# GpSimd makes the product of gate and up, and the product with the block scales, in the feed-forward pass of an adaLN block

## The chip, the cores and the metric

One core of one Trainium2 chip. The metric is the device time of one execution in microseconds, the median of the runs; lower is better. The engines are TensorE (PE), VectorE (DVE), ScalarE (ACT), GpSimd (POOL) and SyncE (SP), which issues all DMAs here. Everything is float32.

## What is computed

`x` is 16 sequences (batches) of 512 tokens with 128 features. A modulation vector per batch scales and shifts two normalised inputs: one of an attention block (chunked ridge attention with a rank-8 subspace), one of a feed-forward block with blockwise FP4 quantisation. The change touches the feed-forward block:

```
def fp4_quant_dequant(x):            # blocks of 16 along the last dim
    scale = max(max|xb| / 6, 1e-12)
    q = GRID[searchsorted(MID, |xb / scale|)] * sign * scale

gate = fp4_linear(h, w_gate)         # 128 -> 352
y    = fp4_linear(h, w_up)           # 128 -> 352
out  = fp4_linear(silu(gate) * y, w_down)   # quantised again, 352 -> 128
x    = x + gb * out
```

with `h = layernorm(x) * (1 + cb) + sb`.

## The kernel before

The kernel runs three passes one after the other. `front_pass` makes the modulation and the normalised inputs of attention; `attention_pass` makes the attention block and, towards its end, the quantised feed-forward inputs of the first 12 batches; `ffn_pass` makes the feed-forward inputs of the last 4 batches (its "hidden" group, `HiddenInput`) and then the feed-forward block of all 16.

In `ffn_pass` one batch is a tile of 128 partitions x 4 token groups (NC), each with 352 hidden features (FI) in 22 blocks of 16. A batch goes through these steps:

- `gate_up(b)`: TensorE transposes the input (L648), ScalarE copies it out of PSUM (L601), TensorE multiplies with gate and up weights, token group by token group (L654, L655), in two PSUM banks each. ScalarE empties each with Silu into `sg` (L606) and with Copy into `up` (L607), which increments `up_ok`. TensorE may fill a bank again when ScalarE has emptied it.
- `combine(b)` on VectorE: waits for four `up_ok` of batch b, makes `hh = sg * up` (L697, 128x1408), then quantises `hh` in place in two halves of 704 elements with `fp4_blocks`: the largest magnitude of each block (L459), scale (L460), reciprocal (L461), product with it (L462), the rounding step from the exponent bits (L463, L464), add and subtract it (L465, L466), product with the scale (L469), which increments `hhq_ok`, once for each half.
- `down(b)`: TensorE waits for both halves (`hhq_ok`), transposes `hh` in three chunks (L663), ScalarE copies each out (L612, in `turned`), TensorE multiplies with the down weights (L670) into `p_y`.
- `finish(b)` on VectorE: waits for `p_y`, multiplies with `gb` (L692) and adds `x` (L693). SyncE stores the result (L566) and then loads the batch three ahead (L560 to L562).

Every engine works through its own instructions in the order in which they are written; semaphores join them. TensorE's and ScalarE's order is gate_up(0), gate_up(1), and then for each b: down(b) (ScalarE: turned(b)), gate_up(b+2). VectorE's order is the hidden group, and then for each b: combine(b), finish(b-1). GpSimd has only the identity, a constant and the reciprocal square root of the hidden group (`hidden.pool`, L118 and L120); after that it has nothing to do in this pass. In the attention pass it makes two elementwise operations of 128x512 for each batch (L1432, L1434).

`sg`, `up`, `hh`, `hht` and `ys` have two buffers, taken in turn by batch; the inputs `x`, `gb` and `h` have four. The scales and the other quantisation buffers have one each, cut in two halves.

Of the kernel before, what the change touches and what calls it, by code (L numbers as in the profile page):

```python
# [29 lines left out]
ALU = mybir.AluOpType  # L30
# [3 lines left out]
P = 128  # L34
B = 16
NC = 4
# [11 lines left out]
FI = 352  # L48
QB = 16
NBF = D // QB  # L50
NBI = FI // QB
# [38 lines left out]
def make_identity(nc, pool, ident, sem, count, value=1.0):  # L90

    nc.gpsimd.memset(ident, 0.0).then_inc(sem, 1)
    pool.wait_ge(sem, count + 1)
    nc.gpsimd.affine_select(out=ident, in_=ident, compare_op=ALU.not_equal, fill=value, base=0,
                            pattern=[[-1, ident.shape[1]]], channel_multiplier=1).then_inc(sem, 1)


def bcast(ap, dim, n):

    a = ap.unsqueeze(dim)  # L100
    shape = list(a.shape)
    shape[dim] = n
    return a.to_broadcast(shape)
# [79 lines left out]
def front_pass(nc, x, ln_g, ln_b, c, wmod, s_mod, s_c, s_xnt, s_base):  # L183

    with ExitStack() as ctx:
# [31 lines left out]
        STORES = 16 * 3  # L217
        LOOPS = (B - 1 - 2) // S

        def batches(eng, step_):  # L220

            step_(0, 0)
            with eng.Fori(0, LOOPS) as k:
                for i in range(S):
                    step_(k * S + (i + 1), (i + 1) % S)
            for b in range(1 + LOOPS * S, B):
                step_(b, b % S)
# [5 lines left out]
        with nc.Block() as block:  # L233
# [133 lines left out]
            def _(dve):  # L367
# [35 lines left out]
                def step_(b, s):  # L403
                    if exists(b, 2):
                        stats(b + 2, (s + 2) % S, 0)
                    if exists(b, 1):
                        make_h(b + 1, (s + 1) % S)
                        stats(b + 1, (s + 1) % S, 1)
                    product = make_base(b, s)
                    if exists(b, 2):  # L410
                        neg_mean(b + 2, (s + 2) % S, 0)
                    make_xn(b, s, product)
                    if exists(b, 1):
                        neg_mean(b + 1, (s + 1) % S, 1)
# [17 lines left out]
                first = ch.n  # L432
                with dve.Fori(0, LOOPS) as k:
                    ch.base, ch.n = k * (S * STEP_LINKS), first
                    for i in range(S):
                        step_(k * S + (i + 1), (i + 1) % S)
                    assert ch.n - first == S * STEP_LINKS, ch.n - first
                ch.base, ch.n = LOOPS * (S * STEP_LINKS), first
                for b in range(1 + LOOPS * S, B):
                    step_(b, b % S)  # L440

def fp4_blocks(nc, ch, jobs):

    last = {}  # L450

    def each(instruction, first=False):
        for k, job in enumerate(jobs):
            if not first:
                ch.wait(last[k])
            last[k] = ch.inc(instruction(*job[:5]))

    V = nc.vector
    each(lambda v, amax, scale, inv, step: V.tensor_reduce(amax, v, op=ALU.max, axis=AX_X, apply_absolute_value=True), first=True)  # L459
    each(lambda v, amax, scale, inv, step: V.tensor_scalar(scale, amax, 1.0 / 6.0, 1e-12, ALU.mult, ALU.max))  # L460
    each(lambda v, amax, scale, inv, step: V.reciprocal(inv, scale))  # L461
    each(lambda v, amax, scale, inv, step: V.tensor_tensor(v, v, bcast(inv, 2, QB), ALU.mult))  # L462
    each(lambda v, amax, scale, inv, step: V.tensor_scalar(step.bitcast(I32), v.bitcast(I32), 0x7F800000, None, ALU.bitwise_and))  # L463
    each(lambda v, amax, scale, inv, step: V.tensor_scalar(step, step, 1.0, 1.5 * 2.0 ** 22, ALU.max, ALU.mult))  # L464
    each(lambda v, amax, scale, inv, step: V.tensor_tensor(v, v, step, ALU.add))  # L465
    each(lambda v, amax, scale, inv, step: V.tensor_tensor(v, v, step, ALU.subtract))  # L466
    for k, (v, amax, scale, inv, step, done) in enumerate(jobs):
        ch.wait(last[k])
        V.tensor_tensor(v, v, bcast(scale, 2, QB), ALU.mult).then_inc(done, 1)  # L469


def fp4_weights(nc, ch, v, rows, nb, tmp):
# [25 lines left out]
def ffn_pass(nc, s_wgu, s_wdn, s_mod, s_x1, s_h, out):  # L498


    with ExitStack() as ctx:
        sb = lambda name, shape, dt=F32: ctx.enter_context(nc.sbuf_tensor("m_" + name, shape, dt))
        ps = lambda name, shape: ctx.enter_context(nc.psum_tensor("m_" + name, shape, F32))
        sem = lambda name: ctx.enter_context(nc.semaphore("m_" + name))
# [7 lines left out]
        S = 4  # L512
# [4 lines left out]
        sg = [sb(f"sg{s}", [P, NC, FI]) for s in range(2)]  # L517
        up = [sb(f"up{s}", [P, NC, FI]) for s in range(2)]
        hh = [sb(f"hh{s}", [P, NC, FI]) for s in range(2)]
        hht = [sb(f"hht{s}", [P, NW, NC, P]) for s in range(2)]  # L520
        ys = [sb(f"y{s}", [P, NC, D]) for s in range(2)]
        q_hh = [sb(n, [P, NC * NBI]) for n in ("amax", "scale", "inv")] + [sb("step", [P, NC * FI])]
        late_x, late_md = sb("late_x", [P, GB_N, NC, D]), sb("late_md", [P, GB_N, 2, D])
        late_step, late_small = sb("late_step", [P, GB_N * NC * D]), sb("late_small", [P, 2 * BANK])
        hidden = HiddenInput(nc, sem, [late_x[:]], [late_md[:]], late_step[:], lambda at, n: late_small[:, at:at + n], nhalf[:])
# [7 lines left out]
        x_in = [sem(f"x_in{s}") for s in range(S)]  # L533
        saved = [sem(f"saved{s}") for s in range(2)]
        nhalf_ok, dve_chain, passed = (sem(n) for n in ("nhalf_ok", "dve_chain", "passed"))
        ht_mm, ht_ok, gate_mm, up_ok, hh_ok, hhq_ok, hht_mm, hht_ok, y_mm, y_ok = (
            sem(n) for n in ("ht_mm", "ht_ok", "gate_mm", "up_ok", "hh_ok", "hhq_ok", "hht_mm", "hht_ok", "y_mm", "y_ok"))

        AHEAD = 3
        LOOPS = (B - 1 - AHEAD) // S  # L540

        def batches(eng, step_):

            step_(0, 0)
            with eng.Fori(0, LOOPS) as k:
                for i in range(S):
                    step_(k * S + (i + 1), (i + 1) % S)
            for b in range(1 + LOOPS * S, B):
                step_(b, b % S)

        def exists(b, ahead):

            return not isinstance(b, int) or b + ahead < B

        with nc.Block() as block:
# [34 lines left out]
            @block.gpsimd  # L590
            def _(pool):
                make_identity(nc, pool, ident[:], ident_ok, 0)
                nc.gpsimd.memset(nhalf[:], -0.5).then_inc(nhalf_ok, 1)
                pool.wait_ge(nhalf_ok, 1)
                hidden.pool(pool, 0)

            @block.scalar
            def _(act):
# [84 lines left out]
            @block.vector  # L683
            def _(dve):
                ch = Chain(dve, dve_chain)
                for s in range(2):
                    dve.sem_inc(saved[s], 16)

                def finish(b, s):
                    dve.wait_ge(y_mm, b + 1)  # L690
                    dve.wait_ge(saved[s % 2], (b - s % 2) * 8 + 16)
                    ch.link(nc.vector.tensor_tensor(ys[s % 2][:], p_y[:], gb[s][:].to_broadcast([P, NC, D]), ALU.mult))  # L692
                    nc.vector.tensor_tensor(ys[s % 2][:], ys[s % 2][:], xs[s][:], ALU.add).then_inc(y_ok, 1)  # L693

                def combine(b, s):
                    dve.wait_ge(up_ok, b * NC + NC)
                    nc.vector.tensor_tensor(hh[s % 2][:], sg[s % 2][:], up[s % 2][:], ALU.mult).then_inc(hh_ok, 1)  # L697
                    dve.wait_ge(hh_ok, b + 1)
                    jobs = []
                    for half in range(2):  # L700
                        nb = NC * NBI // 2
                        amax, scale, inv = (x[:, half * nb:(half + 1) * nb] for x in q_hh[:3])
                        v = hh[s % 2][:, half * NC // 2:(half + 1) * NC // 2].rearrange("p t (b k) -> p (t b) k", k=QB)
                        step = q_hh[3][:, half * nb * QB:(half + 1) * nb * QB].rearrange("p (b k) -> p b k", k=QB)
                        jobs.append((v, amax, scale, inv, step, hhq_ok))
                    fp4_blocks(nc, ch, jobs)


                STEP_LINKS = 2 * 8 + 1

                def step_(b, s):
                    combine(b, s)
                    if not isinstance(b, int) or b >= 1:
                        finish(b - 1, (s - 1) % S)

                hidden.vector(dve, ch, 0, 0, passed)
                step_(0, 0)
                first = ch.n
                with dve.Fori(0, LOOPS) as k:
                    ch.base, ch.n = k * (S * STEP_LINKS), first  # L720
                    for i in range(S):
                        step_(k * S + (i + 1), (i + 1) % S)
                    assert ch.n - first == S * STEP_LINKS, ch.n - first
                ch.base, ch.n = LOOPS * (S * STEP_LINKS), first
                for b in range(1 + LOOPS * S, B):
                    step_(b, b % S)
                finish(B - 1, (B - 1) % S)
# [898 lines left out]
```

## Time and profile before

| what | us |
|---|---|
| median of 3 runs | 1955.35 |
| lowest and highest | 1954.31, 1958.24 |
| span of the profiled execution | 1955.5 |
| VectorE busy | 1637.0 (84%) |
| TensorE busy | 1111.4 (57%) |
| ScalarE busy | 796.1 (41%) |
| GpSimd busy | 120.1 (6%) |
| mean granted TensorE clock | 0.767 |
| first instruction of the down product's pass on batch 0 (L663) | at 1736.91 |

The span is the time from the first to the last instruction of one profiled execution, and the busy shares are of that span. The timeline lists instructions in order of time, with their start and duration in us; like instructions are merged, with their count behind x. What stands in brackets is the idle time of the engine before them and what ended it. In the answers on windows, each stretch has its length, the busy time of PE, PEld (TensorE's weight loads), DVE, ACT and POOL with their instruction counts, the granted TensorE clock (1.00 is 2.4 GHz, 0.50 is 1.2 GHz), the DMA share and GB/s.

### The profile page before, as it was taken

The page shows a single profiled execution, that of the slowest core. Times are in us where ns is not written, and L with a number is a line of the kernel's source. Part 1 is how long each engine was busy: PE and PEld are TensorE (multiplying, and loading weights), DVE is VectorE, ACT ScalarE, POOL GpSimd, SP SyncE. Part 2 cuts the span into 40 slices and gives each one's busy share as a digit, 9 for nine tenths or more (in the row PEclk, how much of TensorE's full clock was granted, in tenths as well). Part 3 has the DMA queues.
Part 4 walks back from the last instruction along what each step waited for, and adds up shares of the span by engine and source line. Part 5 has one row for each costly group of instructions (what it writes and reads, how often), then busy time and mean ns, then how long its engine had stood idle before and what let it go on. Part 6 is the DMA issues. An engine that isn't in the chain of part 4 may idle for free. (4 is left out here: it accounts for less than half of the span.)

```text
span 1955.5 us, 54893 instructions
## 1 busy us (share of the span) xinstructions
PE 1111.4 (57%) x21470; PEld 912.4 (47%) x21470; DVE 1637.0 (84%) x5229; ACT 796.1 (41%) x1499; POOL 120.1 (6%) x119
## 2 busy tenths in 40 slices
PE   2438201891662876776486867377407717347876
PEld 1325101851552863575485456277306616235554
DVE  6865799699999489999939999976998970399997
ACT  3645100652541553673354465255406404124342
POOL 3530000000000002000001100000201000200000
PEclk6659655695895688898669889758758959579998
DMA  2551000000000002100000200000121110411220
GB/s 91 173 182 57 27 0 0 15 29 12 3 3 1 4 3 81 35 4 3 2 4 24 81 2 4 2 3 4 61 78 43 39 39 2 132 51 57 66 64 28
DMA packets 58236, 73.85 MB, mean 38 GB/s; under 512 B 4512, under 2 KB 32880, under 8 KB 57984
## 3 DMA queue, kind: packets, MB, share of 16 engines
q1 hardware_dynamic: 57984, 70.38, 11.4%
q8 instruction: 172, 2.82, 0.6%
q14 instruction: 80, 0.66, 0.1%
HBM read 44.61 MB, written 25.76 MB: 36 GB/s over the span
## 5 line engine op out<-in xcount | busy, mean ns | idle before, releaser
L1500 DVE TENSOR_TENSOR a_blocks<-a_blocks,a_outer 128x384 f32<-128x384 f32 (+3 forms) x1024 | 455.3, 487 | 0.0
L1494 DVE TENSOR_TENSOR a_outer<-a_blocks,a_scaled 128x128 f32<-128x128 f32 (+3 forms) x1024 | 440.7, 492 | 2.0 <-DVE a_blocks L1528 1.3
L1150 ACT ACTIVATE a_pair<-a_bank 32x512 f32<-32x512 f32 (+1 forms) x352 | 207.2, 592 | 205.6 <-PE a_bank L932 126.5
L932 PE MATMUL a_bank<-a_ident,a_blocks 128*128 128x128 f32 x256 | 46.8, 367 | 366.7 <-DVE a_blocks L1510 366.7
L1150 ACT ACTIVATE a_work<-a_bank 32x512 f32<-32x512 f32 (+1 forms) x224 | 130.7, 589 | 294.5 <-PE a_bank L932 222.9
L932 PEld LDWEIGHTS a_bank<-a_ident,a_blocks 128*128 128x128 f32 x256 | 45.3, 214 | 368.3 <-DVE a_blocks L1510 197.8
L883 PE MATMUL a_bank<-a_wk,a_cg 128*128 128x512 f32 x256 | 123.6, 630 | 11.5 <-issue 11.5
L951 PE MATMUL a_bank<-a_work,a_gram 64*32 64x32 f32 (+1 forms) x4096 | 105.8, 220 | 17.9 <-issue 14.7
L951 PEld LDWEIGHTS a_bank<-a_work,a_gram 64*32 64x32 f32 (+1 forms) x4096 | 98.6, 135 | 23.4 <-issue 21.4
L1150 ACT ACTIVATE a_xb<-a_bank 128x512 f32<-128x512 f32 x112 | 63.4, 596 | 112.4 <-PE a_bank L1056 63.8
L1432 POOL TENSOR_TENSOR a_xc<-a_xc,a_ga 128x512 f32<-128x512 f32 x16 | 23.2, 1453 | 1358.2 <-ACTq L1155 1311.6
L1150 ACT ACTIVATE a_xa<-a_bank 128x512 f32<-128x512 f32 x112 | 62.3, 604 | 65.2 <-PE a_bank L1056 43.7
L1563 DVE TENSOR_TENSOR a_basis<-a_basis,a_dinv 128x512 f32<-128x512 f32 x8 | 5.2, 688 | 91.4 <-PEq L1099 91.4
L883 PEld LDWEIGHTS a_bank<-a_wk,a_cg 128*128 128x128 f32 x256 | 48.8, 200 | 68.0 <-issue 61.8
L1056 PE MATMUL a_bank<-a_pair,a_ya 64*8 64x64 f32 x4096 | 51.9, 227 | 45.8 <-issue 35.0
L895 PEld LDWEIGHTS a_bank<-a_pair,a_wk 128*64 128x64 f32 x1024 | 55.5, 137 | 38.1 <-ACT a_pair L1150 38.1
L109 DVE BATCH_NORM_STATS2 m_late_small<-m_late_x 128x6 f32<-128x128 f32 x16 | 3.4, 274 | 83.2 <-DMA m_late_md<-s_mod 83.2
L895 PE MATMUL a_bank<-a_pair,a_wk 128*64 128x128 f32 x1024 | 62.1, 275 | 16.0 <-ACT a_pair L1150 16.0
L951 PE MATMUL a_bank<-a_pair,a_work 64*32 64x64 f32 x2048 | 68.0, 224 | 5.1 <-issue 4.1
L951 PEld LDWEIGHTS a_bank<-a_pair,a_work 64*32 64x32 f32 x2048 | 62.8, 111 | 7.5 <-issue 5.9
L1056 PEld LDWEIGHTS a_bank<-a_pair,a_ya 64*8 64x8 f32 x4096 | 42.1, 86 | 48.5 <-issue 48.1
L351 PE MATMUL f_pt<-f_ident,f_xn 128*128 128x128 f32 x64 | 17.4, 425 | 79.9 <-DVE f_xn L398 77.7
(212 smaller groups left out, 2625.5 us busy)
## 6 DMA issues: line engine op xcount, KB each, us to landing
f_x<-in_L_attn_x SPq DMA_DIRECT2D x16, 256.0 KB, 3.2
s_xnt<-f_xt SPq DMA_DIRECT2D x16, 256.0 KB, 2.1
s_c<-f_cm SPq DMA_DIRECT2D x16, 256.0 KB, 2.3
s_base<-f_base SPq DMA_DIRECT2D x16, 256.0 KB, 2.8
a_cg<-s_c SPq DMA_DIRECT2D x16, 256.0 KB, 2.7
a_cc<-s_c SPq DMA_DIRECT2D x16, 256.0 KB, 3.6
a_xnt<-s_xnt SPq DMA_DIRECT2D x16, 256.0 KB, 3.7
a_base_in<-s_base SPq DMA_DIRECT2D x16, 256.0 KB, 2.7
```

What stands on the lines that cost most here:

```text
L109: ch.inc(nc.vector.bn_stats(raw[:, t], x[:, t]))
L351: last = nc.tensor.transpose(p_t[s % 2][:, t], ns[s][:, t], ident[:])
L883: last = nc.tensor.matmul(bank[:], cg[bb % 2][:, 2 * (tp % 2) + i], wk[:, 8 * half:8 * half + 8, :].rearrange("p h d -> p (h d)"), start=T ...
L895: last = nc.tensor.matmul(bank[rows(s, None), i * P:(i + 1) * P].rearrange("p (t c) -> p t c", t=2), wk[:, h, :], ck[tp % 2][:, :, h * DH: ...
L932: last = nc.tensor.transpose(bank[:, i * P:(i + 1) * P], rows_[:, :, 4 * jb + i], ident[:])
L951: last = nc.tensor.matmul(two[s][at(s), i * w:(i + 1) * w], stationary, moving, start=True, stop=True)
L1056: last = nc.tensor.matmul(two[s][32 * c:32 * c + R, i * DH:(i + 1) * DH], src[rows(s, None), q, :], pair[rows(s, None), q, :], start=True, ...
L1150: nc.scalar.activation(out, view, ACT.Copy, scale=scale).then_inc(emptied, 1)
L1432: nc.gpsimd.tensor_tensor(y, y, ga[:].to_broadcast([P, NC, D]), ALU.mult).then_inc(pool_chain, 1)
L1494: made[a] = ch.inc(V.tensor_tensor(outer[a // KEPT], bcast(factor, 3, HB - a), bcast(scaled[:, :, a:HB], 2, KEPT), ALU.mult))
L1500: differences = ch.inc(V.tensor_tensor(strip, strip, outer[a // KEPT], ALU.subtract))
L1563: last = V.tensor_tensor(basis[:, :, s], basis[:, :, s], bcast(dinv[:, s], 2, DH), ALU.mult)
```

## The change

The product of gate and up moves from VectorE to GpSimd, and so does the last step of the quantisation, the product with the scales. VectorE's `combine` becomes `quantise`, which waits for GpSimd's product (`hh_ok`), rounds both halves, and increments `rounded` once for each half. GpSimd's step b makes the product of batch b+1 and then, for each half of batch b, waits for `rounded` and multiplies with the scale; product 0 comes before the first step. The scales get two buffers, taken in turn by batch. All other engines keep their order.

```
--- before.py
+++ after.py
@@ -441,7 +441,7 @@
 
 
 
-def fp4_blocks(nc, ch, jobs):
+def fp4_blocks(nc, ch, jobs, rounded=None):
 
 
 
@@ -466,7 +466,10 @@
     each(lambda v, amax, scale, inv, step: V.tensor_tensor(v, v, step, ALU.subtract))
     for k, (v, amax, scale, inv, step, done) in enumerate(jobs):
         ch.wait(last[k])
-        V.tensor_tensor(v, v, bcast(scale, 2, QB), ALU.mult).then_inc(done, 1)
+        if rounded is None:
+            V.tensor_tensor(v, v, bcast(scale, 2, QB), ALU.mult).then_inc(done, 1)
+        else:
+            ch.eng.sem_inc(rounded, 1)
 
 
 def fp4_weights(nc, ch, v, rows, nb, tmp):
@@ -519,7 +522,8 @@
         hh = [sb(f"hh{s}", [P, NC, FI]) for s in range(2)]
         hht = [sb(f"hht{s}", [P, NW, NC, P]) for s in range(2)]
         ys = [sb(f"y{s}", [P, NC, D]) for s in range(2)]
-        q_hh = [sb(n, [P, NC * NBI]) for n in ("amax", "scale", "inv")] + [sb("step", [P, NC * FI])]
+        q_amax, q_inv, q_step = sb("amax", [P, NC * NBI]), sb("inv", [P, NC * NBI]), sb("step", [P, NC * FI])
+        q_scale = [sb(f"scale{s}", [P, NC * NBI]) for s in range(2)]
         late_x, late_md = sb("late_x", [P, GB_N, NC, D]), sb("late_md", [P, GB_N, 2, D])
         late_step, late_small = sb("late_step", [P, GB_N * NC * D]), sb("late_small", [P, 2 * BANK])
         hidden = HiddenInput(nc, sem, [late_x[:]], [late_md[:]], late_step[:], lambda at, n: late_small[:, at:at + n], nhalf[:])
@@ -533,11 +537,18 @@
         x_in = [sem(f"x_in{s}") for s in range(S)]
         saved = [sem(f"saved{s}") for s in range(2)]
         nhalf_ok, dve_chain, passed = (sem(n) for n in ("nhalf_ok", "dve_chain", "passed"))
+        rounded = sem("rounded")
         ht_mm, ht_ok, gate_mm, up_ok, hh_ok, hhq_ok, hht_mm, hht_ok, y_mm, y_ok = (
             sem(n) for n in ("ht_mm", "ht_ok", "gate_mm", "up_ok", "hh_ok", "hhq_ok", "hht_mm", "hht_ok", "y_mm", "y_ok"))
 
         AHEAD = 3
         LOOPS = (B - 1 - AHEAD) // S
+
+        def half_of(s, half):
+
+            nb = NC * NBI // 2
+            v = hh[s % 2][:, half * NC // 2:(half + 1) * NC // 2].rearrange("p t (b k) -> p (t b) k", k=QB)
+            return v, q_scale[s % 2][:, half * nb:(half + 1) * nb]
 
         def batches(eng, step_):
 
@@ -593,6 +604,24 @@
                 nc.gpsimd.memset(nhalf[:], -0.5).then_inc(nhalf_ok, 1)
                 pool.wait_ge(nhalf_ok, 1)
                 hidden.pool(pool, 0)
+
+                def product(b, s):
+                    pool.wait_ge(up_ok, b * NC + NC)
+                    nc.gpsimd.tensor_tensor(hh[s % 2][:], sg[s % 2][:], up[s % 2][:], ALU.mult).then_inc(hh_ok, 1)
+
+                def rescale(b, s):
+                    for half in range(2):
+                        pool.wait_ge(rounded, b * 2 + (half + 1))
+                        v, scale = half_of(s, half)
+                        nc.gpsimd.tensor_tensor(v, v, bcast(scale, 2, QB), ALU.mult).then_inc(hhq_ok, 1)
+
+                def step_(b, s):
+                    if exists(b, 1):
+                        product(b + 1, (s + 1) % S)
+                    rescale(b, s)
+
+                product(0, 0)
+                batches(pool, step_)
 
             @block.scalar
             def _(act):
@@ -692,24 +721,22 @@
                     ch.link(nc.vector.tensor_tensor(ys[s % 2][:], p_y[:], gb[s][:].to_broadcast([P, NC, D]), ALU.mult))
                     nc.vector.tensor_tensor(ys[s % 2][:], ys[s % 2][:], xs[s][:], ALU.add).then_inc(y_ok, 1)
 
-                def combine(b, s):
-                    dve.wait_ge(up_ok, b * NC + NC)
-                    nc.vector.tensor_tensor(hh[s % 2][:], sg[s % 2][:], up[s % 2][:], ALU.mult).then_inc(hh_ok, 1)
+                def quantise(b, s):
                     dve.wait_ge(hh_ok, b + 1)
                     jobs = []
                     for half in range(2):
                         nb = NC * NBI // 2
-                        amax, scale, inv = (x[:, half * nb:(half + 1) * nb] for x in q_hh[:3])
-                        v = hh[s % 2][:, half * NC // 2:(half + 1) * NC // 2].rearrange("p t (b k) -> p (t b) k", k=QB)
-                        step = q_hh[3][:, half * nb * QB:(half + 1) * nb * QB].rearrange("p (b k) -> p b k", k=QB)
-                        jobs.append((v, amax, scale, inv, step, hhq_ok))
-                    fp4_blocks(nc, ch, jobs)
+                        amax, inv = (x[:, half * nb:(half + 1) * nb] for x in (q_amax, q_inv))
+                        v, scale = half_of(s, half)
+                        step = q_step[:, half * nb * QB:(half + 1) * nb * QB].rearrange("p (b k) -> p b k", k=QB)
+                        jobs.append((v, amax, scale, inv, step, None))
+                    fp4_blocks(nc, ch, jobs, rounded)
 
 
                 STEP_LINKS = 2 * 8 + 1
 
                 def step_(b, s):
-                    combine(b, s)
+                    quantise(b, s)
                     if not isinstance(b, int) or b >= 1:
                         finish(b - 1, (s - 1) % S)
 
```

## Rows read from the trace of the kernel before

**Rows 1.** The page: the span, and each engine's busy time.
```profile
span 1955.5 us, 54893 instructions
...
PE 1111.4 (57%) x21470; PEld 912.4 (47%) x21470; DVE 1637.0 (84%) x5229; ACT 796.1 (41%) x1499; POOL 120.1 (6%) x119
```

**Rows 2.** The chain of waits in the last pass: start us, us, what.
```profile
1753.02 1.64 DVE m_hh L697
...
1764.42 0.88 DVE m_hh L469
...
1930.54 1.55 DVE m_hh L697
```

**Rows 3.** The timeline of VectorE over one batch.
```profile
1766.54 1.62 DVE L697 TENSOR_TENSOR m_hh<-m_sg,m_up 128x1408 f32<-128x1408 f32 x1
...
1768.20 1.68 DVE L459 TENSOR_REDUCE m_amax<-m_hh 128x44 f32<-128x704 f32 x2
...
1777.13 1.69 DVE L469 TENSOR_TENSOR m_hh<-m_hh,m_scale 128x704 f32<-128x704 f32 x2
...
1778.73 0.68 DVE L692 TENSOR_TENSOR m_y<-m_py,m_gb 128x512 f32<-128x512 f32 x1
...
1780.06 1.62 DVE L697 TENSOR_TENSOR m_hh<-m_sg,m_up 128x1408 f32<-128x1408 f32 x1
```

**Rows 4.** The same timeline: the down product and the last evacuation of gate and up.
```profile
1768.10 2.94 PE L670 MATMUL m_py<-m_w_dn,m_hht 128*128 128x128 f32 x24 [0.68 <-ACT m_hht L612]
...
1777.64 0.46 ACT L607 ACTIVATE m_up<-m_pu 128x352 f32<-128x352 f32 x1
```

**Rows 5.** The timeline of GpSimd in the attention pass, its last group.
```profile
1660.37 1.26 POOL L1432 TENSOR_TENSOR a_xc<-a_xc,a_ga 128x512 f32<-128x512 f32 x1 [112.33 <-ACTq L1155]
1661.71 1.26 POOL L1434 TENSOR_TENSOR a_xc<-a_xc,a_base_in 128x512 f32<-128x512 f32 x1
```

**Rows 6.** The timeline of VectorE and GpSimd, attention pass: a meeting, and the same alone.
```profile
743.70 2.76 DVE L1494 TENSOR_TENSOR a_outer<-a_blocks,a_scaled 128x384 f32<-128x384 f32 x4
744.26 1.46 POOL L1432 TENSOR_TENSOR a_xc<-a_xc,a_ga 128x512 f32<-128x512 f32 x1 [600.56 <-ACTq L1155]
...
755.74 1.70 DVE L1494 TENSOR_TENSOR a_outer<-a_blocks,a_scaled 128x384 f32<-128x384 f32 x4
```

**Rows 7.** Windows and the timeline of TensorE at the last batch.
```profile
1934.90:1942.70 7.80, 0.00 (x0) 0.00 (x0) 7.80 (x13) 0.00 (x0) 0.00 (x0) 0.63 0.00 0
1942.70:1949.00 6.30, 5.54 (x24) 4.86 (x25) 1.31 (x3) 1.79 (x3) 0.00 (x0) 0.50 0.14 42
...
1942.78 2.89 PE L663 MATMUL m_phht<-m_ident,m_hh 128*128 128x128 f32 x12 [7.89 <-DVE m_hh L469]
...
1946.35 4.95 PE L670 MATMUL m_py<-m_w_dn,m_hht 128*128 128x128 f32 x24 [0.68 <-ACT m_hht L612]
```

**Rows 8.** The timeline of the first batch after the hidden group.
```profile
1735.16 1.69 DVE L469 TENSOR_TENSOR m_hh<-m_hh,m_scale 128x704 f32<-128x704 f32 x2
...
1736.91 2.89 PE L663 MATMUL m_phht<-m_ident,m_hh 128*128 128x128 f32 x12 [22.80 <-DVE m_hh L469]
...
1740.48 5.47 PE L670 MATMUL m_py<-m_w_dn,m_hht 128*128 128x128 f32 x24 [0.68 <-ACT m_hht L612]
...
1747.77 0.76 PE L655 MATMUL m_pu<-m_w_gu,m_ht 128*128 128x352 f32 x2
...
1752.53 0.46 ACT L607 ACTIVATE m_up<-m_pu 128x352 f32<-128x352 f32 x1
```

**Rows 9.** The timeline of gate and up of batches 0 and 1.
```profile
1703.17 1.38 PE L654 MATMUL m_pg<-m_w_gu,m_ht 128*128 128x352 f32 x2
...
1706.37 0.76 PE L654 MATMUL m_pg<-m_w_gu,m_ht 128*128 128x352 f32 x2
...
1708.11 0.46 ACT L607 ACTIVATE m_up<-m_pu 128x352 f32<-128x352 f32 x1
...
1714.51 0.46 ACT L607 ACTIVATE m_up<-m_pu 128x352 f32<-128x352 f32 x1
```

## The prediction

> **What bounds the kernel now.** The page comes first: VectorE is busy 84% of a span of 1955.5 us, TensorE 57%, GpSimd 6% [rows 1]. These are averages over three passes, and the change touches only the last one, so the chain of waits of that pass is read next. It shows what the engines hand each other batch by batch: the chain comes back to the product of gate and up (L697) at 1753.02 for batch 2 and at 1930.54 for batch 15 [rows 2]. These thirteen steps take 177.5 us, 13.65 each; an ordinary one is 13.52.
>
> The timeline of VectorE in one batch shows why [rows 3]. It has no gap: 1.66 us from the product to the first reduction, 8.93 from there to the first product with the scales (L469), 1.60 for the two of those, 1.33 for the finish of the batch before. Sum 13.52. So VectorE sets the period in the middle of the pass.
>
> How much room do the others have? The same batch on TensorE and ScalarE [rows 4]: after the quantised product is complete (L469 ends at 1765.30 [rows 2]), TensorE transposes it, multiplies (L670), and goes on to gate and up of the batch two ahead; ScalarE empties the last bank of that at 1778.10. That is 12.80 us, against a period of 13.52. The reader is to see that this leg, from the end of batch b's rescaling to the end of batch b+2's gate and up, is nearly as long as the period. It is hidden only because it runs beside VectorE's work on batch b+1.
>
> **The change, part by part.**
>
> *VectorE is relieved* of 1.66 + 1.60 = 3.26 us a batch; for the new completion wait and two semaphore increments I give back 0.1. It would need 10.36 us a batch.
>
> *GpSimd's prices.* The trace has no GpSimd product of 1408 or 704 elements. The nearest are the 128x512 products of the attention pass, 1.26 us undisturbed, the one that follows through a semaphore 0.08 after the end of the first [rows 5]. When such an operation meets VectorE, four VectorE products that take 1.70 alone take 2.76 [rows 6]: 1.06 us is shut-out, which I take as the part that grows with the size, and 0.20 as fixed. Then 1408 elements cost 2.75 x 1.06 + 0.20 = 3.12 us, 704 elements 1.375 x 1.06 + 0.20 = 1.66. With everything growing in proportion they would be 3.47 and 1.73; with the fixed part only they could not be less than 3.12 and 1.66. I take the low ones. L1432 has an operand repeated over whole rows of 128, L1434 none, both 1.26; repetition inside blocks of 16 is in no row, and at worst I let it double the rescale.
>
> *The order on GpSimd* is the step that decides. Its step b first waits for all of gate and up of batch b+1 and makes product b+1, and only then rescales batch b. GpSimd takes its work in order, so the rescale of b, however early VectorE has rounded it, stands behind that wait. And gate and up of b+1 is issued on TensorE behind down(b-1), which waits for the rescale of b-1. That closes a loop with one batch per turn: rescale b-1 done, down(b-1), gate and up of b+1, product b+1, rescale b. In the kernel before, TensorE's leg lay beside VectorE's work on the batch in between; now nothing on GpSimd lies beside it. VectorE's quantising of b is no part of the loop: it starts when product b is there, some 3.5 us ahead of the loop's start, and ends long before product b+1. Who waits: TensorE for the rescale, VectorE for product b+1, SyncE's stores and ScalarE behind TensorE.
>
> GpSimd's share of a turn: 0.08 + 3.12 + 0.08 + 1.66 + 0.08 + 1.66 = 6.68 us. With the leg at 12.80 the turn would be 19.48.
>
> *The clock of that leg.* In every turn TensorE would idle during GpSimd's share and ScalarE's last two evacuations (0.46 each, L607 in rows 4), about 7.6 us. The trace has one idle time of that length behind busy work: 7.89 us before the last batch. The granted clock averages 0.63 in it and is 0.50 when the work resumes; the 24 products of L670 take 4.95 us [rows 7] where they take 2.94 at full clock [rows 4]. The first batch, too, begins at half clock, after 22.80 us of idleness: L469 ends at 1736.85, L670 takes 5.47, and then gate and up runs at full clock to 1752.99 [rows 8]. That leg is 16.14 us, 3.34 more, and it is the pattern I expect in each turn: down at 1.2 GHz, gate and up at 2.4. The turn is 16.14 + 6.68 = 22.82 us.
>
> *Contention.* At product b+1 VectorE has nothing to do, and the rescale of b meets the two reductions of b+1 and then its first two-input product. I cost this at nothing inside the loop; if the two took turns for VectorE's products, it would add 0.8 us a turn.
>
> The Trainium skill (SBUF — State Buffer, Who interferes with whom) says that a VectorE instruction with two SBUF inputs and a GpSimd instruction that reads SBUF shut each other out for a whole instruction, and that reductions don't. The trace agrees for the first half, 2.76 against 1.70 us. By that rule alone the change would give the third rival below; by the order on GpSimd it gives 22.82 a turn, and the shut-outs fall where VectorE idles.
>
> **The sum**, on the profiled execution. Batches 0 and 1 have gate and up ready at 1708.57 and 1714.97 [rows 9], while VectorE still prepares the last group. The two early products shut VectorE out there by 0 to 2 x 2.92; I take 3.7, since part falls on a reduction. VectorE's first product (1.65) goes. Rounding of batch 0 ends at 1735.16 - 1.65 + 3.7 = 1737.2, and the rescale (0.08 + 1.66 + 0.08 + 1.66 = 3.48) ends at 1740.7; before, that was 1736.85. Fourteen turns, for b = 1 to 14: + 319.5, 2060.2. Batch 15 has no product behind it: its quantising starts 3.48 before that, takes 8.93 and one shut-out of 1.46, and its rescale 3.48: + 10.4, 2070.6. After so short a gap I take full clock for its down: 5.74 (1765.30 to 1771.04 in rows 2 and 4), then 4.2 as before from the end of L670 at 1951.30 to the end [rows 7]. Total 2080.5, say 2081, 125 us over the span. The profiled span stands 0.15 us from the median of the runs, so nothing is corrected.
>
> **The rivals.**
>
> *The loop with TensorE at full clock.* If idle times of 7.6 us don't lower the clock, the turn is 19.48 and the end 2034. Against it: the fall inside 7.89 us.
>
> *The loop with gate and up at half clock too.* A pair of L654 takes 1.38 us before the clock rises and 0.76 after [rows 9]; eight pairs of L654 and L655 add 5.0, the turn is 27.8, the end 2151. Against it: the clock had risen when gate and up ran, 11 us after the work's resumption: a pair of L655 takes 0.76 there [rows 8].
>
> *Contention decides, not order.* If gate and up of b+1 came early enough, VectorE's 10.36 plus at most 2.92 + 2 x 1.46 of shut-outs would be 16.2 us a batch, 2.7 more than now, and 15 batches end at 1996. For it speaks the 1.06 us per operation; against it the order.
>
> *Faster.* If the rescale never stood behind a wait, VectorE at 10.36 would cease to bind and TensorE's leg of 12.80 would: 0.7 less in fourteen batches, 1945. It takes gate and up of b+1 to be there before VectorE has rounded b. That is so for batches 0 and 1 only; from b = 2 the leg is 12.8 behind the rescale of b-1 and rounding b is done about 7 behind it.
>
> *GpSimd dearer in blocks of 16.* Doubled rescales add 3.3 a turn: 2130.
>
> **How the numbers follow.** Forecast 0.66, full clock 0.10, half clock throughout 0.07, contention 0.04, faster 0.03, dearer rescale 0.10. The forecast's own range is 2055 to 2105: 0.3 a turn less for an earlier rise of the clock, the start without shut-outs; 0.5 more for products in proportion and 0.8 for turns with VectorE. The range 2030 to 2135 takes in full clock and the dearer rescale and leaves out 0.14. The measurement tells 0.2%, about 4 us. Faster 0.03, same 0.01, slower 0.96.
>
> **What would show it.** GpSimd's timeline: product, rescale, rescale back to back, then idle for some 16 us on ScalarE's L607, with periods near 22.8; products near 3.1 us, rescales near 1.7. L663 waits for GpSimd, L459 too, VectorE idle nearly half of each period. L670 near 5.4 us and L654 pairs near 0.76. Wrong would be: rescales that start right when VectorE has rounded; periods below 17 us; L670 at 2.9; GpSimd operations stretched beyond 4 us beside busy VectorE.

## The result, and the profile after

The changed kernel takes 2049.47 us (median of 4 runs, 2046.22 to 2050.12) against 1956.0 for the kernel before (median of 4; the table of the time before has three of them): a ratio of 1.0483, 95% interval 1.0465 to 1.0501. It is slower by 4.8%, some 94 us. The forecast was 2081 with a range of 2030 to 2135. The span of the profiled execution is 2047.9 us.

First the page of the changed kernel, span and busy time, against [rows 1]:

```profile
span 2047.9 us, 54959 instructions
...
PE 1117.3 (55%) x21470; PEld 917.8 (45%) x21470; DVE 1605.9 (78%) x5181; ACT 797.5 (39%) x1499; POOL 215.4 (11%) x167
```

VectorE is busy for 31 us less (time in which one of its instructions is held up by GpSimd counts as busy), GpSimd for 95 us more, and the span is 92 us longer. The work that was moved is off the engine that bound the pass; what grew is waiting. The waits of the last pass say which engine waits for which (each line names the engine and line that waited, then the engine and line waited for, then us in total, times, longest):

```profile
POOL m_hh L610 <- ACT m_up L636: 207.2, 14, 16.1
DVE m_amax L459 <- POOL m_hh L610: 118.7, 14, 8.9
...
PE m_phht L692 <- POOL m_hh L616: 100.2, 15, 6.9
```

In the changed kernel L610 is GpSimd's product, L616 its rescale, L692 the transposes (L663 before), L699 the down product (L670), L636 the last evacuation (L607). GpSimd waits 14 times for ScalarE, 207.2 us in all; meanwhile VectorE waits 118.7 us for GpSimd's product and TensorE 100.2 for its rescale. The timeline of GpSimd gives the order of events:

```profile
1816.26 3.15 POOL L610 TENSOR_TENSOR m_hh<-m_sg,m_up 128x1408 f32<-128x1408 f32 x1 [15.48 <-ACT m_up L636]
1819.37 2.73 POOL L616 TENSOR_TENSOR m_hh<-m_hh,m_scale 128x704 f32<-128x704 f32 x2
1835.87 3.15 POOL L610 TENSOR_TENSOR m_hh<-m_sg,m_up 128x1408 f32<-128x1408 f32 x1 [13.77 <-ACT m_up L636]
1838.97 2.73 POOL L616 TENSOR_TENSOR m_hh<-m_hh,m_scale 128x704 f32<-128x704 f32 x2
1857.21 3.15 POOL L610 TENSOR_TENSOR m_hh<-m_sg,m_up 128x1408 f32<-128x1408 f32 x1 [15.51 <-ACT m_up L636]
1860.32 2.73 POOL L616 TENSOR_TENSOR m_hh<-m_hh,m_scale 128x704 f32<-128x704 f32 x2
```

Product, rescale, rescale, back to back, and then a wait of 15.5 or 13.8 us for L636. In these fourteen turns the rescale of a batch never starts when VectorE has rounded it; it starts when the product of the next batch ends. Products start 19.6 and 21.3 us apart, in turn; the fourteen turns from the end of rescale 0 at 1737.97 (1734.72 + 3.25) to the end of rescale 14 at 2026.79 (2024.06 + 2.73) average 20.63.

TensorE and the evacuations in two successive turns, to be set beside [rows 3, 4, 8]:

```profile
1822.23 2.88 PE L692 MATMUL m_phht<-m_ident,m_hh 128*128 128x128 f32 x12 [6.90 <-POOL m_hh L616]
...
1825.79 2.94 PE L699 MATMUL m_py<-m_w_dn,m_hht 128*128 128x128 f32 x24 [0.68 <-ACT m_hht L641]
...
1835.33 0.46 ACT L636 ACTIVATE m_up<-m_pu 128x352 f32<-128x352 f32 x1
...
1841.83 2.88 PE L692 MATMUL m_phht<-m_ident,m_hh 128*128 128x128 f32 x12 [6.89 <-POOL m_hh L616]
...
1845.40 4.67 PE L699 MATMUL m_py<-m_w_dn,m_hht 128*128 128x128 f32 x24 [0.68 <-ACT m_hht L641]
...
1856.68 0.46 ACT L636 ACTIVATE m_up<-m_pu 128x352 f32<-128x352 f32 x1
```

and the granted clock where the two differ (length, busy time of PE, PEld, DVE, ACT and POOL, then the clock):

```profile
1824.00:1825.00 1.00, 1.00 (x5) 0.64 (x4) 1.00 (x3) 0.60 (x1) 0.00 (x0) 0.50 0.03 8
1825.00:1826.00 1.00, 0.32 (x2) 0.21 (x2) 1.00 (x3) 0.59 (x1) 0.00 (x0) 0.93 0.07 16
...
1838.00:1839.00 1.00, 0.00 (x0) 0.00 (x0) 0.00 (x0) 0.00 (x0) 1.00 (x2) 0.90 0.00 0
1839.00:1840.00 1.00, 0.00 (x0) 0.00 (x0) 0.95 (x2) 0.00 (x0) 1.00 (x2) 0.50 0.00 0
...
1848.00:1849.00 1.00, 1.00 (x7) 1.00 (x7) 0.98 (x2) 0.00 (x0) 0.00 (x0) 0.50 0.00 0
1849.00:1850.00 1.00, 1.00 (x10) 1.00 (x10) 0.00 (x0) 0.00 (x0) 0.00 (x0) 0.98 0.00 0
```

TensorE comes back at half clock in both turns: the transposes take 2.88 us, as in [rows 7, 8]. In the first the clock is up again by 1826, before L699, which takes 2.94; in the second it rises at 1849, and L699 takes 4.67. The leg from the rescale's end to the last evacuation's end is 13.69 us (1822.10 to 1835.79) and 15.44 (1841.70 to 1857.14).

### The profile page after: what moved, and what is told of

Same layout as the page of the kernel before. It is cut to its first block and busy times, and to the rows that moved or that the text cites. A ratio compares the mean times of both kernels' runs of the same rounds, so it can differ in the third digit from the quotient of the medians.

```text
span 2047.9 us, 54959 instructions
## 1 busy us (share of the span) xinstructions
PE 1117.3 (55%) x21470; PEld 917.8 (45%) x21470; DVE 1605.9 (78%) x5181; ACT 797.5 (39%) x1499; POOL 215.4 (11%) x167
## 3 DMA queue, kind: packets, MB, share of 16 engines
q1 hardware_dynamic: 57984, 70.38, 10.8%
## 5 line engine op out<-in xcount | busy, mean ns | idle before, releaser
L1459 POOL TENSOR_TENSOR a_xc<-a_xc,a_ga 128x512 f32<-128x512 f32 x16 | 21.6, 1349 | 1357.1 <-ACTq L1182 1311.3
L459 DVE TENSOR_REDUCE m_amax<-m_hh 128x44 f32<-128x704 f32 x32 | 26.9, 880 | 119.1 <-POOL m_hh L610 118.7
L692 PE MATMUL m_phht<-m_ident,m_hh 128*128 128x128 f32 (+1 forms) x192 | 46.2, 426 | 126.1 <-POOL m_hh L616 126.1
L692 PEld LDWEIGHTS m_phht<-m_ident,m_hh 128*128 128x128 f32 (+1 forms) x192 | 35.3, 211 | 138.7 <-issue 89.4
L641 ACT ACTIVATE m_hht<-m_phht 128x512 f32<-128x512 f32 (+1 forms) x48 | 28.6, 596 | 143.9 <-PE m_phht L692 143.9
L610 POOL TENSOR_TENSOR m_hh<-m_sg,m_up 128x1408 f32<-128x1408 f32 x16 | 52.1, 3259 | 217.6 <-ACT m_up L636 217.6
```

Of the source, the lines that this page charges most:

```text
L610: nc.gpsimd.tensor_tensor(hh[s % 2][:], sg[s % 2][:], up[s % 2][:], ALU.mult).then_inc(hh_ok, 1)
L641: nc.scalar.activation(hht[s % 2][0:n, k], p_hht[(NW * s + k) % 2][0:n], ACT.Copy).then_inc(hht_ok, 1)
L692: last = nc.tensor.transpose(p_hht[(NW * s + k) % 2][0:n, t], hh[s % 2][:, t, at:at + n], ident[:])
```

## Experiments

Each ratio is to the kernel before, run on the same chip beside it (medians 1953.8 to 1954.5); the numbers before "batch" or "turn" are from the profiled execution.

**1. The order of the two jobs.** GpSimd rescales batch b before it makes product b+1.

```diff
                 def step_(b, s):
+                    rescale(b, s)
                     if exists(b, 1):
                         product(b + 1, (s + 1) % S)
-                    rescale(b, s)
```

> GpSimd's two jobs of a step change places: it rescales batch b first and makes product b+1 after it. Theory (the order closes a loop through TensorE): the loop q(b-1), gate and up of b+1, product b+1, rescale b is gone. Another, shorter one takes its place, because product b+1 now stands behind VectorE's rounding of b: product 3.15, rounding 8.93, two rescales 2.8 and hand-offs, 15.1 a turn, so the whole near 1978 (1968 to 1990). Rival (GpSimd's work costs this much wherever it stands, by its own length or by shutting VectorE out): no change from the changed kernel, 2049.

Measured: 1980.14 us, ratio 1.0128 (1.0111 to 1.0144). 69 of the 94 us go by exchanging two calls. GpSimd's timeline shows the shorter loop that remains, 15.41 us a turn on average (15.2 where the product follows the rescales at once, 15.5 to 15.8 where it also waits 0.2 to 0.6 us for L636):

```profile
1809.44 3.70 POOL L616 TENSOR_TENSOR m_hh<-m_hh,m_scale 128x704 f32<-128x704 f32 x2 [8.38 <-DVEq L472]
1813.10 3.16 POOL L610 TENSOR_TENSOR m_hh<-m_sg,m_up 128x1408 f32<-128x1408 f32 x1
1824.64 3.70 POOL L616 TENSOR_TENSOR m_hh<-m_hh,m_scale 128x704 f32<-128x704 f32 x2 [8.38 <-DVEq L472]
```

It rescales as VectorE finishes rounding: from the product's start to the first rescale's start are 11.54 us, product and rounding one behind the other, and 3.66 more to the next product. VectorE idles between its finish and the next product. GpSimd does the same work in both kernels, so neither its length nor its price on VectorE makes the 94 us wherever that work stands. Its 5.8 us are in every turn of the changed kernel because its queue puts them behind the leg.

**2. The loop opened elsewhere.** The order on GpSimd stays as changed; TensorE and ScalarE make gate and up three batches ahead, with four buffers for `sg`, `up` and `hh`. The diff shows one place; the other engine's step has the same edit, both engines begin with three `gate_up`, and ScalarE waits for an older product before it overwrites a buffer.

```diff
-                    if exists(b, 2):
-                        gate_up(b + 2, (s + 2) % S)
+                    if exists(b, 3):
+                        gate_up(b + 3, (s + 3) % S)
```

> The changed kernel with gate and up made three batches ahead in place of two, and four buffers for sg, up and hh; GpSimd's order stays. Theory (order): product b+1 no longer waits for the rescale of b-1, only for that of b-2, so the one-batch loop opens; what is left is TensorE's leg of 12.8 us and VectorE's 10.4 plus shut-outs (0 to 5.9): 12.8 to 16.2 a batch, I expect 14.5 and 1970 (1945 to 1996). Rival (GpSimd's length or the half clock by itself): 2049 or near it.

Measured: 1949.69 us, ratio 0.9971 (0.9960 to 0.9983). The whole loss is gone, and 0.3% more. I had expected 14.5 us a batch; from 1818 on it is 13.44 (product starts at 1818.07 and 1831.51):

```profile
1827.84 3.71 POOL L616 TENSOR_TENSOR m_hh<-m_hh,m_scale 128x704 f32<-128x704 f32 x2 [6.62 <-DVEq L472]
...
1830.22 1.67 DVE L459 TENSOR_REDUCE m_amax<-m_hh 128x44 f32<-128x704 f32 x2
...
1831.51 3.15 POOL L610 TENSOR_TENSOR m_hh<-m_sg,m_up 128x1408 f32<-128x1408 f32 x1
...
1831.81 2.98 DVE L460 TENSOR_SCALAR m_scale<-m_amax 128x44 f32<-128x44 f32 x2
...
1834.74 0.71 DVE L461 RECIPROCAL m_inv<-m_scale 128x44 f32<-128x44 f32 x2
```

Here the shut-out takes over. The two small L460 take 2.98 us instead of 0.30: they stand behind the product at GpSimd, which began 0.30 us before them. The reductions (1.67 us) run beside the rescale unhindered. In five earlier turns the product meets another instruction and holds that: L462, 4.0 to 4.4 us instead of 1.62, or L463, 3.9 instead of 0.95. VectorE saves 3.26 us a batch and gives back 2.68 here and most of the rest in the wait for its last rounding and in the addition of the finish.

**3. The depth by itself.** The kernel before with three batches ahead, all products on VectorE (the same edit as in 2, on the kernel before).

> The kernel before, with gate and up three batches ahead and four buffers for sg, up and hh, all products on VectorE. It tells whether the 0.3% that the changed kernel gains with three ahead over the kernel before comes from GpSimd's work or from the depth. Theory: VectorE's 13.52 a batch stays the period, and only its 4.2 us of waits for L607 go: 1951 (1949 to 1954), so that moving the two products is worth no more than 2 us. Rival (the depth alone does nothing): 1955, and the products on GpSimd are worth 5.

Measured: 1949.91 us, ratio 0.9978 (0.9965 to 0.9992), the same as in 2. Each of the two ratios is to the kernel before on its own chip. So with a queue that doesn't block, and in this order of VectorE's work, the two products on GpSimd are worth nothing that can be measured: what VectorE saves it loses in shut-outs and small waits.

**4. Each half alone.** First the product alone: VectorE keeps L469, GpSimd's step holds only `product(b + 1)`.

> Only the product moves to GpSimd, one batch ahead; VectorE keeps the product with the scales. Theory (order): nothing on GpSimd stands behind the wait for gate and up, so no one-batch loop. Two batches then cost the leg 12.8, product 3.2, and VectorE's 10.5, 13.3 each, and with the product's shut-out on VectorE 13.8: 1960 (1950 to 1975). Rival (each product on GpSimd adds its length): 15 times 3.1, half of the loss, near 2002.

Measured: 1967.47 us (1963.15 to 1975.32), ratio 1.0077 (1.0050 to 1.0105), an ordinary batch 14.1 us. That is 7 us above the expected 1960, in its range. The timeline of VectorE shows where the product lands; L718 is the finish's addition, 0.69 us in the kernel before:

```profile
1804.27 0.68 DVE L717 TENSOR_TENSOR m_y<-m_py,m_gb 128x512 f32<-128x512 f32 x1
1804.98 2.94 DVE L718 TENSOR_TENSOR m_y<-m_y,m_x 128x512 f32<-128x512 f32 x1
1807.85 1.67 DVE L459 TENSOR_REDUCE m_amax<-m_hh 128x44 f32<-128x704 f32 x2
```

The PSUM product L717 runs beside GpSimd's product (which began at 1804.02), the addition of two SBUF tiles waits 2.25 us for it, in 11 of the 16 batches. The shut-out works the other way too: where VectorE's two-input products were under way first, GpSimd's product took 4.95 to 4.97 us instead of 3.15 (three batches). Then the rescale alone, VectorE keeping the product:

> The other half alone: only the product with the scales is on GpSimd; VectorE keeps the product of gate and up, two ahead as before. Theory (the loss is in the order of the two jobs on one queue): GpSimd waits for rounded batches only, so there is no one-batch loop. VectorE saves 1.60 and loses what of the rescale's 2.8 us meets the addition of the finish and the product of the next batch, some 2.1: 14.1 a batch, 1965 (1955 to 1975). With the 1967 of the product alone, the halves cost some 13 and 10 us, and both together 94. Rival (each half has its share of the 94): near 2035.

Measured: 1957.99 us, ratio 1.0020 (1.0007 to 1.0033). The expectation of 1965 was 7 us too high, though in its range: the shut-out took 0.6 to 0.9 us of the next product (2.22 and 2.55 us against 1.62) and 0.15 of the addition, since most of the rescale lay beside the end of the rounding and the PSUM product. What else is left of the 1.60 that VectorE saves goes in waits, 0.22 for its own last rounding and 0.51 for the last evacuation in the second of these two batches; an ordinary batch takes 13.56. Together the halves cost 17 us, both at once 94. The rest belongs to neither half alone; experiment 1 shows that most of it hangs on their order in one queue.

**5. The shut-out by itself.** The kernel before, and GpSimd makes a 128x1408 product in three buffers of its own, triggered by the end of VectorE's product.

```diff
...
+                def step_(b, s):
+                    pool.wait_ge(hh_ok, b + 1)
+                    pool.wait_ge(bystander, b + 2)
+                    nc.gpsimd.tensor_tensor(d_out[:], d_in[0][:], d_in[1][:], ALU.mult).then_inc(bystander, 1)
...
```

> The kernel before, with all its own work where it was; GpSimd makes, when a batch's product is complete, one product of 128x1408 in buffers of its own that nobody reads. It is the shut-out measured by itself: no engine waits for GpSimd. Theory: GpSimd's product (3.15 us) meets the two reductions first, 1.6 us that it doesn't hold up, and then holds the next VectorE instruction, L460, for the rest, 1.3 us a batch: 1976 (1970 to 1982). Rivals: all of VectorE is held, 2.9 us a batch, 2001; or nothing is, 1955.

Measured: 1977.76 us, ratio 1.0128 (1.0111 to 1.0144). Nothing waits for this product and it shares no buffer, and yet a batch takes 15.07 us instead of 13.52:

```profile
1801.25 1.68 DVE L459 TENSOR_REDUCE m_amax<-m_hh 128x44 f32<-128x704 f32 x2
1802.85 1.82 DVE L460 TENSOR_SCALAR m_scale<-m_amax 128x44 f32<-128x44 f32 x2
1804.61 0.71 DVE L461 RECIPROCAL m_inv<-m_scale 128x44 f32<-128x44 f32 x2
```

The reductions are untouched, L460 takes 1.82 instead of 0.30 us. Its end, 1804.67, is 3.29 us after the product began at 1801.38.

**6. The clock.** The changed kernel, and TensorE makes transposes of the identity before it waits for the rescale. They are extra work into a bank that is free.

```diff
+                    if exists(b, 1) and not (isinstance(b, int) and b == 0):
+                        for i in range(FILL):
+                            nc.tensor.transpose(p_ht[:, i % NC], ident[:], ident[:])
                     pe.wait_ge(hhq_ok, b * 2 + 2)
...
```

With 44 of them:

> The changed kernel, and TensorE makes 44 transposes of the identity into the free bank of the input transposes before it waits for the rescaled product; they are extra work that nothing reads. Theory: the legs are 13.7 and 15.4 us in turn because the clock is 1.2 GHz when TensorE resumes; with the idle time filled the clock stays at 2.4 GHz and each leg is 12.8: turns of 18.7, 1.75 less than now in 14 turns, 2025 (2018 to 2032). Rival (the leg is long for another reason, the granted clock only accompanies it): 2049, or more by what the filler delays.

Measured: 2049.39 us, ratio 1.0482 (1.0463 to 1.0502), no change: the expectation failed. The timeline tells why: in five turns the clock stayed up, in the others it fell, both after 2.1 us of idleness before the transposes (L697 here, and L704 the down product; in the first pair of lines it fell):

```profile
1801.27 2.56 PE L697 MATMUL m_phht<-m_ident,m_hh 128*128 128x128 f32 x12 [2.13 <-POOL m_hh L616]
1804.51 4.82 PE L704 MATMUL m_py<-m_w_dn,m_hht 128*128 128x128 f32 x24 [0.68 <-ACT m_hht L641]
...
1822.45 1.09 PE L697 MATMUL m_phht<-m_ident,m_hh 128*128 128x128 f32 x8 [2.12 <-POOL m_hh L616]
...
1825.11 2.94 PE L704 MATMUL m_py<-m_w_dn,m_hht 128*128 128x128 f32 x24 [0.68 <-ACT m_hht L641]
```

GpSimd's products then start 18.7 us apart where the clock held, 21.2 and 21.6 where it fell. The mean was the old one, so this run by itself decides nothing. With 58 transposes:

> As the run with 44 transposes of filler, with 58, which leaves TensorE some 0.5 us of idle time before the rescaled product in place of 2.1. The turns of that run in which the clock stayed up took 18.7 us, the others 21.2 to 21.6. Theory (the clock makes the leg longer): with less idle time it stays up in more turns, towards 18.7 in all: 2025 (2020 to 2040). Rival (filler doesn't hold the clock, or delays the work by as much as it saves): 2049.

Measured: 2027.99 us, ratio 1.0374 (1.0356 to 1.0392). The turns are alike now:

```profile
1790.40 3.17 POOL L610 TENSOR_TENSOR m_hh<-m_sg,m_up 128x1408 f32<-128x1408 f32 x1 [12.88 <-ACT m_up L636]
1793.53 2.73 POOL L616 TENSOR_TENSOR m_hh<-m_hh,m_scale 128x704 f32<-128x704 f32 x2
1809.13 3.18 POOL L610 TENSOR_TENSOR m_hh<-m_sg,m_up 128x1408 f32<-128x1408 f32 x1 [12.87 <-ACT m_up L636]
...
1827.88 3.17 POOL L610 TENSOR_TENSOR m_hh<-m_sg,m_up 128x1408 f32<-128x1408 f32 x1 [12.87 <-ACT m_up L636]
...
1846.63 3.17 POOL L610 TENSOR_TENSOR m_hh<-m_sg,m_up 128x1408 f32<-128x1408 f32 x1 [12.89 <-ACT m_up L636]
```

18.74 us each, the 12.80 of [rows 2, 4] plus GpSimd's 5.9. The granted clock (after the busy times) is 1.00 in both stretches, to 2000 us:

```profile
1790.00:1850.00 60.00, 53.09 (x379) 44.55 (x377) 34.13 (x55) 16.98 (x37) 20.97 (x11) 1.00 0.16 48
1850.00:2000.00 150.00, 131.78 (x916) 108.99 (x915) 90.75 (x145) 44.41 (x96) 47.09 (x25) 1.00 0.13 38
```

The lower clock is worth some 21 of the 94 us; the other 73 are the loop at full clock.

**7. A version that beats both.** The runs say what is needed: no job on GpSimd that another waits behind, and GpSimd's work beside VectorE instructions that it doesn't hold up. Three batches ahead, the product stays on VectorE, the rescale goes to GpSimd, and VectorE's step runs:

```
product(b + 1)                       # L697 before
rounding(b)                          # L460 to L466
rounded += 1
gated(b - 1)                         # PSUM product, L692 before
rounded += 1
reductions(b + 1)                    # L459
added(b - 1)                         # L693 before
```

> Three batches ahead, the product on VectorE, the rescale on GpSimd, and VectorE's order changed so that what isn't held up lies beside the rescale: product b+1 before the rounding of b; after the rounding of b the PSUM product of the finish (L692 before), the two reductions of b+1, and then the last addition. Theory (the shut-out is by instruction and reductions and the PSUM product escape it): VectorE's 13.52 less 1.60, plus 0.3 to 0.7, 12.2 to 12.6 a batch, against TensorE's 12.0; 1940 (1934 to 1946), faster than both kernels. Rival (the rescale's 2.8 us are lost on VectorE wherever they lie): 14.8 a batch, 1970.

Measured: 1939.76 us, ratio 0.9933 (0.9915 to 0.9951), 0.7% faster than the kernel before and some 5% faster than the changed one. The depth alone gave 0.2% of it (experiment 3). No run has this order with the rescale on VectorE; since VectorE had no gap in its 13.52 us [rows 3], the order alone leaves it no less to do.

```profile
1849.63 0.68 DVE L752 TENSOR_TENSOR m_y<-m_py,m_gb 128x512 f32<-128x512 f32 x1
1850.23 1.67 DVE L730 TENSOR_REDUCE m_amax<-m_hh 128x44 f32<-128x704 f32 x2
1851.82 1.04 DVE L756 TENSOR_TENSOR m_y<-m_y,m_x 128x512 f32<-128x512 f32 x1
1853.54 1.62 DVE L717 TENSOR_TENSOR m_hh<-m_sg,m_up 128x1408 f32<-128x1408 f32 x1 [0.69 <-ACT m_up L629]
```
```profile
1849.05 3.25 POOL L612 TENSOR_TENSOR m_hh<-m_hh,m_scale 128x704 f32<-128x704 f32 x2 [8.75 <-DVEq L765]
```

The second fence is GpSimd's rescale of the same batch. The PSUM product and both reductions (0.68 and 1.67 us) are as long as alone; only the addition (1.04 against 0.69) feels it. From 1799 to 1912 a batch takes 12.0 to 12.9 us (12.56 on average over the pass), and VectorE waits 0.69 us for L629, the last evacuation. TensorE's own round, where it doesn't wait for the rescale, is 12.06 us (L686, its transposes, at 1840.43 and 1852.49), and 12.80 in the next, in which it waits 0.71 for the load of `h`: now VectorE, TensorE and at times this load bound the pass together.

## Why the prediction was right, and where its sizes were off

**The order on GpSimd** was the step that decided, and it held: one batch per turn, with the leg, the product and both rescales in it (14.80 + 5.83 = 20.63 us a turn). Experiment 1 takes it away on GpSimd, experiment 2 on TensorE, and each removes most or all of the loss while GpSimd does the same work.

**GpSimd's share of a turn** was forecast at 6.68 us and is 5.83 from the product's start, with under 0.1 before it. The product was right, 3.15 against 3.12. The rescales were mis-sized: 1.38 us each in place of 1.66 and a hand-off of 0.08. The prediction called 1.66 the least that a rescale could take, because it gave every instruction the 0.20 us that doesn't grow with the size; a rescale whose semaphore is already there follows the one before with no such part between. Blocks of 16 show no extra cost, so the rival of the dearer rescale is out. This is 0.77 a turn, 10.8 of the 32.6 us by which the sum (2080.5) missed the span.

**The leg at mixed clock** was forecast at 16.14 us plus 0.08; GpSimd's wait is 207.2 / 14 = 14.80. This is the larger miss, 1.42 a turn, 19.9 us. That the clock falls in each turn was right, and so was gate and up at full clock (0.76 us for a pair), which rules out the rival of half clock throughout. Wrong was to take the whole of down at half clock in each turn, as in [rows 8]: L699 took 2.94 us in six of the fourteen turns, 4.62 to 4.72 in seven and 5.33 in the first alone. The first turn, in which GpSimd waits 16.07, is the one that the forecast described, and I gave its length to all. I had two resumptions to go by, and both were of the slow kind. An L670 of 2.9 us was on the list of what would show the prediction wrong; it turned up in these six turns, and it says that the clock's share of the leg, not the loop, was too large.

**The start.** Shut-outs by the early products were 3.4 us (L460 0.77 against 0.23 and L463 4.05 against 1.23 on the hidden group) where I took 3.7. GpSimd was held up as well, by VectorE's 128x2048 instructions: its first two products took 4.04 and 4.05 us, past the 4 us on the same list. That happened only there, where neither was on the path. The rescale of batch 0 ended at 1737.97 against the forecast 1740.7; 1.56 of that is a pass that began earlier in this execution (L118 at 1695.34 against 1696.90). The last batch took 10.3 (2026.79 to 2037.10) against 10.4, and the tail 10.8 against 9.9.

**No contention inside the loop** was right as a cost: VectorE waits while the product runs, and only L460 is held, by the second rescale (1.19 us against 0.30), which delays nobody. The prediction had the first two-input product there, not L460.

**The rivals.** Full clock throughout (2034) is what 58 transposes bring about, 2028, so its arithmetic was good and its condition false. The rival of contention was sized at 16.2 us a batch at most; where the loop is open it is 13.44, because 1.67 us of reductions and the PSUM product aren't held. The faster rival (1945) needed an open loop, and with one the products on GpSimd gave nothing over the depth alone.

**The ranges.** The stated range, 2030 to 2135, holds the 2049.47 because it was drawn to take in full clock; the forecast's own range, 2055 to 2105, misses it. Its lower end doesn't follow from its terms either: 0.3 us in each of 14 turns and a start without shut-outs take 2081 to 2073. The two mis-sized terms erred the same way, 30.7 of the 32.6 us together, so no error hid another.

## What to carry to other kernels

Work on an idle engine is only as early as what stands ahead of it in that engine's queue: before moving two jobs to one queue, follow what the first one waits for, and see whether that waits, through any engine, for the second. If it does, the stages that overlapped now run one after the other: the turn is the whole leg plus the moved work, here 14.80 + 5.83 us where it had been 13.52. Where GpSimd and VectorE run side by side, place GpSimd's SBUF products beside VectorE's reductions, reciprocals and PSUM reads; beside its two-input SBUF instructions and its `tensor_scalar`, count the time in which they meet against what VectorE saves.

## What the runs showed of the hardware

- A GpSimd product delays VectorE's 128x44 `tensor_scalar` with a single SBUF input: two take 1.82 us instead of 0.30 beside a product in buffers that nobody shares (experiment 5), and 2.98 in experiment 2. Reductions (1.67 to 1.68 us for two), a product with one operand in PSUM (0.68 to 0.69), and the reciprocals (0.71 for two, at 1805.44 in experiment 2 beside the GpSimd product that began at 1805.40) keep their length. The Trainium skill (SBUF — State Buffer, Who interferes with whom) says that `tensor_scalar` can enter a mode that takes the ports shared with GpSimd, and that `tensor_reduce` never contends on this chip; the trace agrees with both. I had counted only the instructions with two inputs.
- GpSimd products in a row cost 1.38 us for 704 elements and 3.15 for 1408: 2.0 to 2.2 ns an element, with no visible fixed part between them. VectorE's two-input instructions hold GpSimd up as well: a product of 3.15 us took 4.04 beside 128x2048 ones and 4.95 to 4.97 in three batches of experiment 4.
- The clock fell in a turn in which TensorE had stood still for only 2.1 us before its transposes (experiment 6, 44 transposes), and not in other turns with the same idle time. In the changed kernel, too, like turns differ: the clock rises some 3 us after the transposes begin (1822.23 to 1825.1) or some 7 (1841.83 to 1849.0). What decides between them stays open; it wasn't tried.
